# A recurrent network on one core: ScalarE instead of VectorE rounds the new state's high part in the first two blocks

## The chip, the core and the metric

The kernel runs on one core of a Trainium2 chip. The engines of the core work side by side and are tied together by semaphores only: TensorE (PE in the profile; its weight loads are PEld), VectorE (DVE), ScalarE (ACT), GpSimd (POOL, idle here) and SyncE (SP, which issues the DMAs). The metric is the time of one execution on the device in microseconds (us).

## What is computed

A gated recurrent unit runs over 128 time steps, 64 sequences side by side, with 512 inputs and 512 hidden values. After every fourth step the state that is carried on is a further layer of the new state. The result is x plus the new states. From the reference (it runs through `jax.lax.scan` over the steps):

```python
def step(h, inp):
    x_t, prop = inp
    comb = jnp.concatenate([x_t, h], axis=-1)
    z = jax.nn.sigmoid(comb @ Wz + bz)
    r = jax.nn.sigmoid(comb @ Wr + br)
    comb2 = jnp.concatenate([x_t, r * h], axis=-1)
    h_cand = jnp.tanh(comb2 @ Wh + bh)
    h_new = (1.0 - z) * h + z * h_cand
    h_next = jnp.where(prop, jnp.tanh(h_new @ Wp + bp), h_new)
    return (h_next, h_new)
...
x = x + _L0_cond_ref(x, cond_1024, ...)   # the h_new of all steps
```

## The kernel before

**Numbers as two halves.** Every factor of a product is held as a high and a low part in 16 bits: `h_split[:, :, 0]` is the state rounded to f16 and `h_split[:, :, 1]` is what is left of it. A product is then three: high weights with high values, low weights with high values, high weights with low values. The state lies transposed, as 128 partitions by 4 chunks (`KC`) by 64 sequences (`B`), 256 elements in a partition. Much is done in two halves of two chunks (`HALVES`), 128 elements each.

**The steps.** The 128 steps are 16 blocks of 8. In step t TensorE runs, in this order: the products of gate R with the state (`rec(R, ...)`, line 1122, 48 small matmuls of 64 columns, the first on the first high half), those of gate Z, those of gate C with q = r * h, and then a *fill*: part of the input products of a later block, which does not depend on the state (line 953 in block 0, 512 columns each; `stage`, line 1047, from block 1 on, 256 columns each). Then comes step t + 1. So the fill is what TensorE has to do while the other engines turn the sums of C into the new state. In steps 3, 7, 11, ... (`propagates(t)`) the further layer `PROP` is put between two pieces of fill; there the state's split goes to `q_split` (`p_split`) instead.

**ScalarE in a step** (from line 575): `squash(R)` as two halves (line 504), in steps 2, 4, 5, ... a rounding of weight sums (`split_wsum`, 465) and of input values (`split_slot`, 458), `squash(Z)` as a whole, `squash(C)` as two halves, then `seed(R, t + 1)` and `seed(Z, t + 1)`, which put the input part of the next step's sums into PSUM (524), then reading of finished fills (443, or 470 and 483), then `seed(C, t + 1)`. In step 2 `split_rec(PROP)` (498, two instructions) and the first seed of `PROP` (540) stand ahead of that. Seeds and gates are in the way of one another: an engine takes its instructions in the order written.

**VectorE in a step** (from line 859): `q_split` high as two halves (868), q in full (870), its low part (857), roundings' low parts (714, 706), `keep` = (z - 1) * h (883), `new` = z * c in halves (888), then the new state's high part `new - keep` straight to f16 in halves (898), the same difference in full precision (`h_even` or `h_odd`, 901), the low part (857), and the sum with x, which is the output (909). After that come sums for later blocks (735, 766) and magnitudes of input values (628, 631).

**Who waits.** `h_hi_ready` counts the halves of the high part; TensorE waits for 2t + 1 before the first products of step t and for 2t + 2 sixteen matmuls later. `h_lo_ready` does the same for the low part. `h_new_ready` counts the halves of the full state. Everything here is an order written out by hand; no scheduler moves anything.

## Time and profile before

| | |
|---|---|
| median of 3 runs | 1055.98 us (1055.78 to 1056.47) |
| the profiled execution's own time | 1056.31 us |
| its span in the trace | 1054.5 us |
| busy share: PE, PEld, DVE, ACT | 99%, 92%, 76%, 65% |
| granted TensorE clock | 0.999 |
| instructions: PE, DVE, ACT | 23984, 2692, 1666 |
| the recurrence starts at | 51.14 us |
| step 16 starts at | 175.09 us |

The trace counts time from the span's start. An engine's busy share does not say by itself what bounds the kernel: TensorE's matmuls are pipelined and overlap, so a matmul's duration is longer than what it adds. What it adds is the distance of two starts, 0.029 us for one of 64 columns, 0.109 us for 256 and 0.216 us for 512. PEld, the weight loads, shows better where TensorE is really held up.

### The profile page before, as it was taken

Reading aid. Unit: us, or ns where it says so; the run is one execution under the profiler, and the core shown is the slowest. Engines: PE = TensorE matmul, PEld = TensorE weight load, DVE = VectorE, ACT = ScalarE, POOL = GpSimd, SP = SyncE. Lnnn points to the kernel's source line nnn. Section 1 sums busy time; section 2 is a strip of 40 time slices with the busy share of each in tenths; the row PEclk is TensorE's granted clock in tenths of the full one; section 3 lists DMA queues with packets and bytes.
Section 4 is the critical chain, followed back from the end, with each engine's and each line's share of the span. In section 5 each row is a group of like instructions: output and inputs, shape, how many; then the busy total and the mean of one; then the engine's idle time right before and its main releaser. Section 6 shows DMA issues by size and latency. Waiting matters only on the chain.

```text
span 1054.5 us, 53898 instructions
## 1 busy us (share of the span) xinstructions
PE 1044.9 (99%) x23984; PEld 966.2 (92%) x23984; DVE 799.2 (76%) x2692; ACT 689.4 (65%) x1666; POOL 0.2 (0%) x4
## 2 busy tenths in 40 slices
PE   9999999999999999999999999999999999999997
PEld 3477999999999999999999999999999999999997
DVE  6989988877777777777777777777777776666665
ACT  4766767666666666666666666666675666565664
POOL 0000000000000000000000000000000000000000
PEclk9999999999999999999999999999999999999999
DMA  9312211101111001111001110011110000000001
GB/s 325 110 43 83 77 59 43 44 3 44 43 43 44 23 23 44 43 43 43 21 26 43 44 43 22 24 43 43 43 43 23 24 23 24 23 24 23 24 4 43
DMA packets 38344, 47.63 MB, mean 45 GB/s; under 512 B 2144, under 2 KB 33760, under 8 KB 37728
## 3 DMA queue, kind: packets, MB, share of 16 engines
q1 hardware_dynamic: 38112, 44.19, 12.4%
q8 instruction: 188, 3.08, 1.2%
q14 instruction: 44, 0.36, 0.1%
HBM read 27.40 MB, written 16.78 MB: 42 GB/s over the span
## 4 chain that ended last, share of the span: by engine, by line
PE 94%; DVE 4%; ACT 1%; DMA 1%; issue 1%; SPq 0%; DVEq 0%
PE acc L1122 54%; PE x_acc L1047 34%; PE x_acc L953 5%; PE x_acc L1072 1%; DVE mag L628 1%; DMA x_blk<-x_dram 1%; DVE wrec_lo L692 1%; DVE mag_x L631 0%; DVE win_lo L684 0%; ACT gate L504 0%; DVE x_lo L699 0%; ACT wrec_hi L498 0%; DVE x_lo L706 0%; DVE keep L883 0%; DVE x_blk L909 0%
## 5 line engine op out<-in xcount | busy, mean ns | idle before, releaser
L504 ACT ACTIVATE gate<-acc,unscale 128x128 f32<-128x128 f32 x702 | 239.0, 384 | 268.7 <-PE acc L1122 268.4
L1122 PE MATMUL acc<-h_split,wrec_hi 128*128 128x64 f16 x8192 | 343.8, 193 | 0.0
L1047 PE MATMUL x_acc<-x_hi,win_hi 128*128 128x256 f16 x1092 | 297.7, 273 | 0.0
L1047 PE MATMUL x_acc<-x_hi,win_lo 128*128 128x256 f16 x1092 | 297.6, 273 | 0.0
L1047 PE MATMUL x_acc<-x_lo,win_hi 128*128 128x256 f16 x1092 | 297.6, 273 | 0.0
L1122 PEld LDWEIGHTS acc<-h_split,wrec_hi 128*128 128x128 f16 x8192 | 283.1, 98 | 0.0
L1122 PE MATMUL acc<-q_split,wrec_hi 128*128 128x64 f16 x5088 | 215.5, 193 | 0.0
L1122 PE MATMUL acc<-h_split,wrec_lo 128*128 128x64 f16 x4096 | 203.2, 193 | 1.4 <-DVE h_split L898 1.4
L470 ACT ACTIVATE x_part<-x_acc,bias,part_unscale 128x256 f32<-128x256 f32 x312 | 159.0, 561 | 47.5 <-PE x_acc L1047 47.4
L1122 PEld LDWEIGHTS acc<-q_split,wrec_hi 128*128 128x128 f16 x5088 | 179.2, 98 | 0.0
L524 ACT ACTIVATE acc<-x_part,seed_scale 128x256 f32<-128x256 f32 x384 | 172.7, 477 | 0.1
L1122 PEld LDWEIGHTS acc<-h_split,wrec_lo 128*128 128x128 f16 x4096 | 163.0, 98 | 6.2 <-ACT acc L524 1.5
L1122 PE MATMUL acc<-q_split,wrec_lo 128*128 128x64 f16 x2544 | 126.1, 193 | 1.4 <-DVE q_split L868 1.2
L1047 PEld LDWEIGHTS x_acc<-x_hi,win_lo 128*128 128x128 f16 x1092 | 106.8, 98 | 12.4
L1047 PEld LDWEIGHTS x_acc<-x_hi,win_hi 128*128 128x128 f16 x1092 | 106.8, 98 | 11.0
L1047 PEld LDWEIGHTS x_acc<-x_lo,win_hi 128*128 128x128 f16 x1092 | 106.8, 98 | 10.9
L1122 PEld LDWEIGHTS acc<-q_split,wrec_lo 128*128 128x128 f16 x2544 | 98.0, 98 | 3.3 <-issue 2.6
L868 DVE TENSOR_TENSOR q_split<-gate,h_even 128x128 f16<-128x128 f32 x128 | 35.1, 292 | 73.4 <-ACT gate L504 73.3
L779 DVE SCALAR_TENSOR_TENSOR x_part<-x_acc,part_unscale,x_part 128x512 f32<-128x512 f32 x78 | 58.3, 749 | 30.8 <-ACT x_part L470 15.2
L888 DVE SCALAR_TENSOR_TENSOR new<-gate,scale 128x128 f32<-128x128 f32 x256 | 78.5, 348 | 0.0
L857 DVE TENSOR_TENSOR q_split<-q_full,q_split 128x128 f16<-128x128 f32 x256 | 62.3, 284 | 0.3 <-issue 0.3
L953 PE MATMUL x_acc<-x_lo,win_hi 128*128 128x128 f16 (+2 forms) x224 | 59.9, 288 | 0.0
(116 smaller groups left out, 1059.8 us busy)
## 6 DMA issues: line engine op xcount, KB each, us to landing
out_dram<-x_blk SPq DMA_DIRECT2D x30, 512.0 KB, 3.2
x_blk<-x_dram SPq DMA_DIRECT2D x24, 512.0 KB, 4.2
x_blk<-x_dram SPq DMA_DIRECT2D x3, 1024.0 KB, 8.8
x_blk<-x_dram SPq DMA_DIRECT2D x4, 256.0 KB, 4.0
x_part<-wz_dram SPq DMA_DIRECT2D x4, 256.0 KB, 7.0
x_part<-wh_dram SPq DMA_DIRECT2D x4, 256.0 KB, 6.6
x_part<-wr_dram SPq DMA_DIRECT2D x1, 1024.0 KB, 11.1
x_part<-wz_dram SPq DMA_DIRECT2D x1, 1024.0 KB, 13.3
```

Source lines behind the costliest of these rows:

```text
L470: nc.scalar.activation(part_quarter(m, g, jh, nh)[:, j], in_halves(x_acc[bank][:])[:, j], ACT.Identity, bias=bias[:, g, 2 * jh + j:2 * jh ...
L504: nc.scalar.activation(gate[g][:, half, :], acc[g][:, half, :], func, scale=unscale[:, g:g + 1]).then_inc(gate_ready[g], 1)
L524: nc.scalar.activation(acc[g], added, ACT.Copy, scale=seed_scale[:, g:g + 1]).then_inc(seed_ready[g], 1)
L628: nc.vector.tensor_reduce(mag[:, col:col + 1], src, AX_X, ALU.max, apply_absolute_value=True).then_inc(mag_ready[col], 1)
L692: nc.vector.scalar_tensor_tensor(out=flat(wrec_lo[g][:, rows]), in0=flat(stage_rec[g][:, rows]), scalar=scale[:, g:g + 1], in1=flat(wrec_h ...
L779: nc.vector.scalar_tensor_tensor(out=part_quarter(m, g, jh, 1), in0=in_halves(x_acc[bank][:]), scalar=part_unscale[:, m % 2, g:g + 1], in1 ...
L857: return nc.vector.tensor_tensor(split[:, half, 1, :], full[:, half, :], split[:, half, 0, :], ALU.subtract)
L868: nc.vector.tensor_tensor(q_split[:, half, 0, :], gate[R][:, half, :], h_in[:, half, :], ALU.mult).then_inc(q_hi_ready, 1)
L888: nc.vector.scalar_tensor_tensor(out=new[:, half, :], in0=gate[C][:, half, :], scalar=h_scale, in1=gate[Z][:, half, :], op0=ALU.mult, op1= ...
L953: return nc.tensor.matmul(x_acc[bank][:, 0:cols], weights[g][:, 2 * (j // 2) + k // 2, k % 2, j % 2 * P:(j % 2 + 1) * P], values[m % 2][:, ...
L1047: mm = nc.tensor.matmul(in_halves(x_acc[bank][:])[:, j], weights[g][:, slot_w, k, j * P:(j + 1) * P], in_halves(values[m % 2][:, slot_x, : ...
L1122: mm = nc.tensor.matmul(acc[g][:, j, :], weights[g][:, k, j * P:(j + 1) * P], values[:, k, lo, :], start=False, stop=False, skip_group_che ...
```

## The change

For the twelve steps of the first two blocks that are not followed by the further layer (steps 0, 1, 2, 4, 5, 6, 8, 9, 10, 12, 13, 14):

- VectorE does not make the high part any more (two instructions of line 898 less in each step). It makes the full state right after `new`, then adds x, then waits for both halves of the high part and makes the low part.
- ScalarE waits for both halves of the full state and makes the high part from it in one instruction of 256 elements, f32 to f16. It stands between `seed(R, t + 1)` and `seed(Z, t + 1)`, and counts `h_hi_ready` up by two at once.

In the other 116 steps nothing changes.

```diff
+        def high_by_act(t):
+
+            return t < 2 * BLOCK and not propagates(t)
...
-                if t + 1 < T:
-                    for g in (R, Z):
-                        if g not in late:
-                            seed(g, t + 1)
+                if t + 1 < T and R not in late:
+                    seed(R, t + 1)
+                if high_by_act(t):
+                    act.wait_ge(h_new_ready, 2 * t + 2)
+                    nc.scalar.copy(h_split[:, :, 0, :], h_even_odd[t % 2][:]).then_inc(h_hi_ready, 2)
+                if t + 1 < T and Z not in late:
+                    seed(Z, t + 1)
...
-                if t + 1 < T:
+                if t + 1 < T and not high_by_act(t):
                     for n, half in enumerate(HALVES):
                         dve.wait_ge(new_ready, 2 * t + n + 1)
                         nc.vector.tensor_tensor(split[:, half, 0, :], new[:, half, :], keep[:, half, :], ALU.subtract).then_inc(hi, 1)
...
+                def add_x():
+                    dve.wait_ge(h_new_ready, 2 * t + 2)
+                    nc.vector.scalar_tensor_tensor(out=x_blk[m % RING][:, :, s, :], in0=h_out[:], scalar=h_unscale,
+                                                   in1=x_blk[m % RING][:, :, s, :], op0=ALU.mult, op1=ALU.add).then_inc(out_ready, 1)
+
+                if high_by_act(t):
+                    add_x()
                 if t + 1 < T:
                     for n, half in enumerate(HALVES):
-                        dve.wait_ge(hi, count + n + 1)
+                        dve.wait_ge(hi, count + n + 1 if not high_by_act(t) else count + 2)
                         dve.wait_ge(h_new_ready, 2 * t + n + 1)
                         subtract_hi(h_out, split, half).then_inc(lo, 1)
...
+                if not high_by_act(t):
+                    add_x()
```

ScalarE around the end of step 2, before (L504 gates, L524 seeds, L498 the rounding of the further layer's weights, L540 its seed, L443 a finished fill read):

```order
33 L504 ACTIVATE gate<-acc,unscale 128x256
34 L504 ACTIVATE gate<-acc,unscale 128x128 x2
35 L524 ACTIVATE acc<-x_part,seed_scale 128x256 x2
36 L498 ACTIVATE wrec_hi<-x_blk,scale 128x1024 x2
37 L540 ACTIVATE acc<-prop_bias,seed_scale 128x256
38 L443 ACTIVATE x_part<-x_acc,bias,part_unscale 128x512
39 L524 ACTIVATE acc<-x_part,seed_scale 128x256
40 L504 ACTIVATE gate<-acc,unscale 128x128 x2
```

and after (the same lines have numbers 4 higher):

```order
37 L508 ACTIVATE gate<-acc,unscale 128x256
38 L508 ACTIVATE gate<-acc,unscale 128x128 x2
39 L528 ACTIVATE acc<-x_part,seed_scale 128x256
40 L597 CAST h_split<-h_even 128x4x64
41 L528 ACTIVATE acc<-x_part,seed_scale 128x256
42 L502 ACTIVATE wrec_hi<-x_blk,scale 128x1024 x2
43 L544 ACTIVATE acc<-prop_bias,seed_scale 128x256
44 L447 ACTIVATE x_part<-x_acc,bias,part_unscale 128x512
45 L528 ACTIVATE acc<-x_part,seed_scale 128x256
46 L508 ACTIVATE gate<-acc,unscale 128x128 x2
```

One instruction, the cast, has come in ahead of the seed of Z, and six instructions stand between it and the gate of step 3.

VectorE at the same place, before (L883 `keep`, L888 `new`, L898 the high part, L901 the full state, L857 the low part, L909 the sum with x):

```order
105 L883 SCALAR_TENSOR_TENSOR keep<-gate,h_odd 128x256
106 L888 SCALAR_TENSOR_TENSOR new<-gate,scale 128x128 x2
107 L898 TENSOR_TENSOR h_split<-new,keep 128x2x64 x2
108 L901 TENSOR_TENSOR h_even<-new,keep 128x128 x2
109 L857 TENSOR_TENSOR h_split<-h_even,h_split 128x2x64 x2
110 L909 SCALAR_TENSOR_TENSOR x_blk<-h_even,unscale,x_blk 128x4x64
```

and after:

```order
103 L890 SCALAR_TENSOR_TENSOR keep<-gate,h_odd 128x256
104 L895 SCALAR_TENSOR_TENSOR new<-gate,scale 128x128 x2
105 L908 TENSOR_TENSOR h_even<-new,keep 128x128 x2
106 L911 SCALAR_TENSOR_TENSOR x_blk<-h_even,unscale,x_blk 128x4x64
107 L864 TENSOR_TENSOR h_split<-h_even,h_split 128x2x64 x2
```

The full state has moved up to the place of the high part, and the sum with x ahead of the low part.

ScalarE at the end of step 8, the first of block 1, before (L483 copies a finished product within PSUM, L470 reads another one as two halves):

```order
86 L524 ACTIVATE acc<-x_part,seed_scale 128x256 x2
87 L483 COPY x_acc<-x_acc 128x512
88 L470 ACTIVATE x_part<-x_acc,bias,part_unscale 128x256 x2
89 L524 ACTIVATE acc<-x_part,seed_scale 128x256
90 L504 ACTIVATE gate<-acc,unscale 128x128 x2
```

and after:

```order
98 L528 ACTIVATE acc<-x_part,seed_scale 128x256
99 L597 CAST h_split<-h_even 128x4x64
100 L528 ACTIVATE acc<-x_part,seed_scale 128x256
101 L487 COPY x_acc<-x_acc 128x512
102 L474 ACTIVATE x_part<-x_acc,bias,part_unscale 128x256 x2
103 L528 ACTIVATE acc<-x_part,seed_scale 128x256
104 L508 ACTIVATE gate<-acc,unscale 128x128 x2
```

The cast stands ahead of five instructions that lead up to the gate of step 9.

## Rows read from the trace of the kernel before

**Rows 1.** The page: busy time and share of the span; the chain's shares by engine

```profile
PE 1044.9 (99%) x23984; PEld 966.2 (92%) x23984; DVE 799.2 (76%) x2692; ACT 689.4 (65%) x1666; POOL 0.2 (0%) x4
PE 94%; DVE 4%; ACT 1%; DMA 1%; issue 1%; SPq 0%; DVEq 0%
```

**Rows 2.** Busy time of each engine in stretches of 15 us

```profile
core 0: us, PE busy (x) PEld busy (x) DVE busy (x) ACT busy (x) POOL busy (x), PEclk, DMA share, GB/s
90.00:105.00 15.00, 14.59 (x345) 11.61 (x341) 15.00 (x46) 11.29 (x26) 0.00 (x0) 1.00 0.25 74
195.00:210.00 15.00, 15.00 (x365) 14.38 (x364) 11.76 (x43) 10.57 (x26) 0.00 (x0) 1.00 0.19 62
```

**Rows 3.** Timeline, step 1: start, us, engine, line, xcount [idle before <-releaser]

```profile
60.13 0.62 ACT L504 ACTIVATE gate<-acc,unscale 128x128 f32<-128x128 f32 x2 [0.49 <-PE acc L1122]
60.65 0.48 DVE L868 TENSOR_TENSOR q_split<-gate,h_even 128x128 f16<-128x128 f32 x2
```

**Rows 4.** Timeline of step 2

```profile
67.04 0.63 ACT L504 ACTIVATE gate<-acc,unscale 128x128 f32<-128x128 f32 x2 [0.48 <-PE acc L1122]
67.62 0.48 DVE L868 TENSOR_TENSOR q_split<-gate,h_odd 128x128 f16<-128x128 f32 x2
```

**Rows 5.** Timeline from the end of step 2 to the C products of step 3

```profile
70.70 0.49 DVE L898 TENSOR_TENSOR h_split<-new,keep 128x128 f16<-128x128 f32 x2
70.28 0.87 ACT L524 ACTIVATE acc<-x_part,seed_scale 128x256 f32<-128x256 f32 x2
71.08 2.18 ACT L498 ACTIVATE wrec_hi<-x_blk,scale 128x1024 f16<-128x1024 f32 x2
74.62 0.61 ACT L504 ACTIVATE gate<-acc,unscale 128x128 f32<-128x128 f32 x2
75.02 0.54 DVE L868 TENSOR_TENSOR q_split<-gate,h_even 128x128 f16<-128x128 f32 x2 [0.21 <-ACT gate L504]
75.45 0.39 PE L1122 MATMUL acc<-q_split,wrec_lo 128*128 128x64 f16 x8 [0.45 <-DVE q_split L868]
```

**Rows 6.** Instructions of ScalarE by form, 48 to 170 us: xcount, busy us, mean ns

```profile
L504 ACT ACTIVATE gate<-acc,unscale 128x128 f32<-128x128 f32 x69 | 21.6, 364 | 13.3 <-PE acc L1122 13.1
L524 ACT ACTIVATE acc<-x_part,seed_scale 128x256 f32<-128x256 f32 x47 | 21.1, 476 | 0.0
L470 ACT ACTIVATE x_part<-x_acc,bias,part_unscale 128x256 f32<-128x256 f32 x20 | 10.2, 560 | 3.0 <-PE x_acc L1047 3.0
L465 ACT ACTIVATE win_hi<-sum_b,scale 128x512 f16<-128x512 f32 x6 | 4.3, 718 | 0.0
L483 ACT COPY x_acc<-x_acc 128x512 f32<-128x512 f32 x3 | 1.7, 568 | 1.2 <-PE x_acc L1047 1.2
```

**Rows 7.** Timeline from the end of step 5 to the start of step 6

```profile
93.81 0.49 DVE L898 TENSOR_TENSOR h_split<-new,keep 128x128 f16<-128x128 f32 x2
94.90 0.37 PE L1122 MATMUL acc<-h_split,wrec_lo 128*128 128x64 f16 x7
```

**Rows 8.** Timeline from step 6 to the C products of step 7

```profile
97.22 0.48 DVE L868 TENSOR_TENSOR q_split<-gate,h_odd 128x128 f16<-128x128 f32 x2
101.28 0.48 DVE L898 TENSOR_TENSOR h_split<-new,keep 128x128 f16<-128x128 f32 x2
101.75 0.40 PE L1122 MATMUL acc<-h_split,wrec_lo 128*128 128x64 f16 x8
103.58 0.63 ACT L504 ACTIVATE gate<-acc,unscale 128x128 f32<-128x128 f32 x2 [0.49 <-PE acc L1122]
104.69 0.48 DVE L868 TENSOR_TENSOR q_split<-gate,h_even 128x128 f16<-128x128 f32 x2
105.11 0.36 PE L1122 MATMUL acc<-q_split,wrec_lo 128*128 128x64 f16 x7 [0.52 <-DVE q_split L868]
```

**Rows 9.** Timeline from the end of step 8 to the gate of step 9

```profile
117.24 0.48 DVE L898 TENSOR_TENSOR h_split<-new,keep 128x128 f16<-128x128 f32 x2
117.80 0.40 PE L1122 MATMUL acc<-h_split,wrec_lo 128*128 128x64 f16 x8
116.73 0.57 ACT L483 COPY x_acc<-x_acc 128x512 f32<-128x512 f32 x1
118.00 1.02 ACT L470 ACTIVATE x_part<-x_acc,bias,part_unscale 128x256 f32<-128x256 f32 x2 [0.71 <-PE x_acc L1047]
119.64 0.62 ACT L504 ACTIVATE gate<-acc,unscale 128x128 f32<-128x128 f32 x2 [0.24 <-PE acc L1122]
```

More of the change, by code:

```diff
@@ L901, in _ @@
                     nc.vector.tensor_tensor(h_out[:, half, :], new[:, half, :], keep[:, half, :], ALU.subtract).then_inc(h_new_ready, 1)
+                def add_x():
[4 more added lines that the diff above has]
+                    add_x()
                 if t + 1 < T:
                     for n, half in enumerate(HALVES):
-                        dve.wait_ge(hi, count + n + 1)
+                        dve.wait_ge(hi, count + n + 1 if not high_by_act(t) else count + 2)
                         dve.wait_ge(h_new_ready, 2 * t + n + 1)
                         subtract_hi(h_out, split, half).then_inc(lo, 1)
-                else:
-                    dve.wait_ge(h_new_ready, 2 * t + 2)
-                nc.vector.scalar_tensor_tensor(out=x_blk[m % RING][:, :, s, :], in0=h_out[:], scalar=h_unscale,
-                                               in1=x_blk[m % RING][:, :, s, :], op0=ALU.mult, op1=ALU.add).then_inc(out_ready, 1)
+                if not high_by_act(t):
+                    add_x()
                 if m + 2 < BLOCKS and s == scale_at(m + 2):
```

## The prediction, as it was put on record

> **What bounds the kernel now.** I read the page's busy times and the chain of waits first. The chain that ended last lies on TensorE for 94% and on VectorE for 4% of the span, and the weight loads are busy for 92% [rows 1]. So the time is TensorE's own stream of work, plus the few places at which that stream stands still. Next I read the stretches. From 195 to 210 us, behind the changed steps, the weight loads are busy for 14.38 of 15 us: TensorE is full. From 90 to 105 us, in block 0, VectorE is busy for all 15 us, and the weight loads for 11.61 (partly because that fill has 512 columns for each load) [rows 2]. VectorE is the tight engine there. Yet what counts is where TensorE waits, and that is read from the timeline of its matmuls. The two large standstills ahead of step 16 that come from the state's loop stand before the C products of steps 3 and 7: TensorE is idle for 0.45 and 0.52 us in the page's terms [rows 5, 8]. Measured from start to start, less the 0.029 us that a 64-column matmul takes, it is about 0.61 and 0.68 us. Everything that makes such a place longer or shorter in the first two blocks moves the end by the same amount, since nothing behind them has slack to give.
>
> The two places have different causes. In step 3 the gate of R comes late (74.62 us) because ScalarE works through a row of instructions without a pause, the two roundings L498 of 2.18 us among them. VectorE had been idle for 0.21 us when the gate came [rows 5]. In step 7 the gate had been there since 103.58 us plus 0.36, and q started only at 104.69: VectorE was late by its own queue [rows 8].
>
> **Handing over.** From a gate to q: the first half of the gate starts at 60.13 and takes 0.364 us [rows 3, 6], and q can follow after 0.03 us. In step 3 q follows 0.40 us behind the gate's start; I use 0.40. From VectorE to TensorE: 0.14 us in step 3 (75.02 + 0.29 for one half of q, then 75.45) [rows 5]; I use 0.15, also from ScalarE to TensorE, which no row shows. From VectorE to ScalarE no row of the loop shows it either; I take 0.04, as from ScalarE to VectorE, and 0.15 as the far end.
>
> **The cast's price K.** No row shows a cast on ScalarE. Seeds have the same 256 elements and take 476 ns with one scale operand; L470 has a bias as well and takes 560, so an operand costs some 85 ns, and the cast has none: 476 - 85 = 0.39 us. L483, a copy without operands, takes 568 ns for 512 elements; from 128 to 256 elements gate and seed differ by 112 ns, so that 256 fewer would take off 0.22, leaving 0.35. Bounds: 0.30 below, and 0.57 above, what the copy of twice the size takes; the farthest row, 512 elements from SBUF to SBUF in f16, takes 718 ns [rows 6]. I take 0.39, nearest to the seed's row, which reads SBUF as the cast does. The next instruction of ScalarE starts some 0.08 us before the one ahead ends, as two seeds do (two in 0.87 us, 0.476 each) [rows 5, 6]. On this price the Trainium skill ("VectorE: DVE Perf Modes", section on the TRN2 errata) speaks against many small ScalarE instructions: SBUF sources pay a fixed cost each, 224 cycles plus one per element at 1.2 GHz; an estimate from that page is 480 cycles = 0.40 us, and the sum below would be 0.03 us more. No run so far shows the cast itself.
>
> **When the high part is there now.** The full state takes the place of the high part, so its two halves are done when those of L898 were. Then come 0.04 to ScalarE, K, and 0.15 to TensorE, together 0.19 + K = 0.58 us. What hides this is the fill. Its reserve is the start of the next step's first matmul minus the end of L898. Of the twelve steps it is about 0.96 to 1.06 us in steps 0, 1, 2 and 4 (step 2: L898 ends at 71.19), 1.94 in steps 9, 12 and 14, and 0.60 to 0.64 in steps 5, 10 and 13, of which step 5 is shown (94.90 - 94.30) [rows 5, 7]. In step 6 it is 101.75 - 101.76 = -0.01 and in step 8 it is 117.80 - 117.72 = 0.08 [rows 8, 9]. The first ten are covered, three of them by only 0.02 to 0.06 us; the last two are not.
>
> **The sum, place by place.**
>
> *Steps 1 and 2: a small gain.* q starts at 60.65 and 67.62, while the gates at 60.13 and 67.04 would allow 60.53 and 67.44 [rows 3, 4]. VectorE was late by a magnitude and by scales in its queue, and it now has two instructions of 0.20 us each less ahead of them (0.40 in all for the pair's place). So these gaps go: C starts about 0.09 and 0.17 us earlier. The first is smaller than 0.12, because TensorE's own stream was ready only 0.09 before. Together -0.26 us.
>
> *Step 2 to 3: a loss.* ScalarE had seeded R from 70.28 and Z from 70.68, and started the roundings at 71.08. Now the cast may start only at 71.19 + 0.04 = 71.23, so Z's seed starts at 71.23 + 0.39 - 0.08 = 71.54, 0.86 us later than before. Behind it stand L498 twice, the seed of PROP, a fill's reading, the seed of C and the gate of R for step 3, all back to back [rows 5]. TensorE waits for q, which waits for that gate. The whole 0.86 us is added to the standstill at 75.45. In terms of K: 0.47 + K. Most of it, 0.55 us, is waiting for the full state, not casting.
>
> *Steps 6 and 7: one gap for another.* Step 7's first product comes at 101.76 + 0.58 = 102.34, 0.59 late. VectorE's relief does not help here: q of step 6 was let go by its gate and everything from there to the new state stands behind it [rows 8]. The gate of step 7 is then at 103.58 + 0.59 = 104.17, q at 104.57 instead of 104.69. Before, q was late by VectorE's queue; that queue is about 0.1 shorter now (0.40 saved, 0.3 given back waiting for the cast before the low part). So the gap before C shrinks by more than the new one costs: -0.12, or K - 0.51. Here the old standstill is the cover.
>
> *Steps 8 and 9: a loss.* Step 9 starts at 117.72 + 0.58 = 118.30, 0.50 late, and no old gap takes it up. ScalarE is also behind: the cast starts at 117.76, Z's seed at 118.07, then L483 (0.48 from start to start), L470 twice (0.92) and C's seed (0.40), each seed 0.40. So the gate of R could start at 118.07 + 2.20 = 120.27, while TensorE would allow 119.64 + 0.50 = 120.14 [rows 9]. That is 0.13 more: 0.63 in all, or 0.24 + K.
>
> *The other steps:* nothing on TensorE; the cast and the later Z seed lie beside the fill and the first products of R. The low part comes 0.3 us later or less, and TensorE asks for it 0.9 us behind the first product. No DMA moves on SP's queue; the output's sum is ready earlier.
>
> Sum: -0.26 + 0.86 - 0.12 + 0.63 = **+1.11 us**; with K free, -0.06 + 3K. With K = 0.30 it is 0.8; with 0.57 it is 1.65, and steps 5, 10 and 13 then miss their reserve by some 0.1 each, 2.0 in all. A handover of 0.15 to ScalarE instead of 0.04 adds 0.3. Against the profiled execution's 1056.31 us that is 1057.4; against the median of the runs, which lies 0.33 lower, it is **1057.1 us**.
>
> **Rivals.**
>
> *The relief of the tight engine wins.* VectorE is at 15.00 of 15 us in block 0 [rows 2], loses 12 x 0.40 = 4.8 us of work, and its lateness costs TensorE 0.26 us in steps 1 and 2 and 0.68 in step 7. If the casts disappeared behind the fill, the sum would be -0.9: 1055.1. Against it: the reserve of step 6 is nil and ScalarE has no pause in step 2. The Trainium skill ("Perfetto Trace Analysis", section on optimizing Scalar/DVE operations) has this as a rule: with a saturated VectorE it may make sense to move work to ScalarE. The trace agrees that VectorE is saturated there, but shows the state's path running through both engines. Chance 0.06.
>
> *It changes nothing.* The change is in 12 of 128 steps, and if the handovers are shorter than I took and old gaps absorb the new ones, as in step 7, it is 0 to 0.5 us: 1056.2. Against it: step 9 has no gap to absorb anything. That the change does not do what it says is no separate case: the order shows twelve casts more and 24 subtractions fewer. Chance 0.12.
>
> *The cast is dear.* If it costs what a 512-element rounding takes, 0.72 us, -0.06 + 3K gives 2.1, and the reserves of 0.60 to 0.64 in steps 5, 10 and 13 are missed by about 0.3 each: 3.0 in all, 1059.0, slower beyond what can be told from none. This decides from K of about 0.57 on. For it: no cast was ever seen here, and its f16 output is strided. Against it: gates and seeds agree on a price by element. Chance 0.10.
>
> **How the numbers follow.** The forecast, between 0.7 and 2.0 us of loss, has 0.72. The range takes in the rivals at 1056.2 and, nearly, those at 1055.1 and 1059.0, with the runs' own spread of 0.7 us: 1055.4 to 1058.7. A measurement of this kernel can tell about 0.2%, 2.1 us, from no change. Of the forecast and both lower rivals nearly all lies within that: same 0.88. Slower is the dear cast, 0.10. Faster by 2.1 us would need more than all the standstills that the loop's waits make, 0.02.
>
> **What would show it.** In the profile after: casts of 0.39 us; the C products of step 3 starting 0.6 us later than 75.45, ahead of them step 3 itself earlier by some 0.26; a new wait before the first product of step 7 and none of note before its C products; the same before step 9; from step 10 on a constant shift of about 1.1 us to the end. Wrong would be a shift that grows in steps 10 to 14 (the cast is dear), or one that is negative at step 16 (the relief wins).

## The result and the profile after

The changed kernel takes 1058.38 us (median of 20 runs, 1057.82 to 1058.97), the kernel before, run beside it, 1056.57 us (20 runs, 1055.78 to 1057.18). The ratio is 1.0017, with a 95% interval of 1.0011 to 1.0023: 1.8 us slower, between 1.2 and 2.4. The forecast was 1057.1 us, a loss of 1.1. Of the 1.3 us between forecast and median, 0.6 is no error on the change: the median of before, over 20 runs, lies 0.6 above that of the 3 runs from which the forecast started. The rest, some 0.7 us, is looked for below.

The page of after, its busy times and the chain's shares (in the place of [rows 1]):

```profile
PE 1045.2 (99%) x23984; PEld 966.0 (91%) x23984; DVE 798.0 (76%) x2668; ACT 695.5 (66%) x1678; POOL 0.2 (0%) x4
PE 94%; DVE 3%; ACT 1%; DMA 1%; issue 1%; SPq 0%; ACTq 0%; DVEq 0%
```

VectorE has 24 instructions less and ScalarE 12 more. Their busy time in the stretch of the change, 48 to 170 us (columns as in [rows 2]), before:

```profile
48.00:170.00 122.00, 120.61 (x2789) 104.15 (x2788) 111.33 (x350) 86.24 (x198) 0.00 (x0) 1.00 0.18 57
```

and after:

```profile
48.00:170.00 122.00, 118.97 (x2736) 102.05 (x2735) 107.82 (x321) 88.95 (x207) 0.00 (x0) 1.00 0.18 57
```

VectorE, the tight engine, is busy for 3.5 us less and ScalarE for 2.7 more, and TensorE's weight loads for 2.1 less: TensorE got less done in the same 122 us, so part of the 3.5 us is work that now falls behind the stretch. From the start of step 0 to the start of step 16, the same work in both traces, VectorE is busy for 112.59 us before and 110.62 after, and ScalarE for 85.87 and 90.11: 2.0 us less and 4.2 more. The granted clock is 1.00 in both. The work was moved as said, and the time rose all the same. Where it rose is seen in TensorE's waits. The standstills that TensorE has from 48 to 165 us, by what it waits for (engine, line, waited for: us in total, times, longest), before:

```profile
PE acc L1122 <- DVE q_split L868: 1.2, 3, 0.5
```

and after:

```profile
PE acc L1134 <- DVE q_split L875: 1.6, 2, 1.4
PE acc L1134 <- ACT h_split L597: 0.9, 2, 0.5
PE acc L1134 <- DVE q_split L905: 0.4, 1, 0.4
```

The small waits of steps 1 and 2 are gone, one wait for q has grown to 1.4 us, there are two waits for the cast, and one, for line 905, which the forecast did not have.

To add them up I set the two traces side by side, with the first product of gate R of each step (R) and its first C product (C) as marks, counted from the start of step 0. The table has after minus before in us:

| mark | after - before | place | measured | forecast |
|---|---|---|---|---|
| C of step 2 | -0.25 | steps 1, 2 | -0.25 | -0.26 |
| C of step 3 | +0.67 | step 2 to 3 | +0.92 | +0.86 |
| R of step 7 | +1.35 | first product of 7 | +0.64 | +0.59 |
| C of step 7 | +0.67 | steps 4 to 7, net | 0.00 | -0.12 |
| R of step 8 | +0.96 | within step 7 | +0.29 | 0 |
| R, C of step 9 | +1.53, +1.64 | step 8 to 9 | +0.57, +0.11 | +0.50, +0.13 |
| C of step 14 | +1.76 | step 13 to 14 | +0.11 | 0 |
| R of step 16 | +1.62 | step 15 to 16 | -0.14 | 0 |

The row of step 7's first product counts from R of step 6 (+0.71) and is contained in the net row below it. The sum is 1.62 us at the end of block 1, against 1.11. It stays there within 0.1 us as far as step 60. In this one execution it then grows to 1.94 by step 126; in the kernels below it changes over the same steps by 0.2 us or less. The cause of this growth is open.

**The casts.** ScalarE by form, 48 to 170 us (line, shapes, xcount, busy us, mean ns, idle before), to be read against [rows 6]:

```profile
L597 ACT CAST h_split<-h_even 128x256 f16<-128x256 f32 x8 | 3.3, 407 | 7.0 <-DVE h_even L908 7.0
```

A cast takes 407 ns, where I had put 0.39 us. The estimate of 0.40 us from the Trainium skill ("VectorE: DVE Perf Modes", the TRN2 errata) was nearer by a hair; the trace agrees with that page's price for an SBUF source.

**Step 2 to 3** (timeline: start, us, engine, line, xcount, idle before), in the place of [rows 5]:

```profile
70.53 0.49 DVE L908 TENSOR_TENSOR h_even<-new,keep 128x128 f32<-128x128 f32 x2
71.11 0.41 ACT L597 CAST h_split<-h_even 128x256 f16<-128x256 f32 x1 [0.51 <-DVE h_even L908]
71.42 0.47 ACT L528 ACTIVATE acc<-x_part,seed_scale 128x256 f32<-128x256 f32 x1
71.83 2.18 ACT L502 ACTIVATE wrec_hi<-x_blk,scale 128x1024 f16<-128x1024 f32 x2
75.38 0.61 ACT L508 ACTIVATE gate<-acc,unscale 128x128 f32<-128x128 f32 x2
75.77 0.55 DVE L875 TENSOR_TENSOR q_split<-gate,h_even 128x128 f16<-128x128 f32 x2 [0.21 <-ACT gate L508]
76.20 0.28 PE L1134 MATMUL acc<-q_split,wrec_lo 128*128 128x64 f16 x4 [1.37 <-DVE q_split L875]
```

Read it from the top. The full state ends at 70.53 + 0.49 = 71.02 and the cast starts at 71.11, so the handover is 0.09 us and not 0.04. ScalarE had nothing to do for 0.51 us ahead of the cast, though a seed and two long roundings stood behind it. Then it works on without a pause to the gate at 75.38, which was at 74.62. TensorE waits 1.37 us for q instead of 0.45.

**Steps 6 and 7**, in the place of [rows 8]:

```profile
102.62 0.41 ACT L597 CAST h_split<-h_even 128x256 f16<-128x256 f32 x1 [1.39 <-DVE h_even L908]
103.17 0.39 PE L1134 MATMUL acc<-h_split,wrec_lo 128*128 128x64 f16 x8 [0.54 <-ACT h_split L597]
...
107.97 0.61 DVE L895 SCALAR_TENSOR_TENSOR new<-gate,scale 128x128 f32<-128x128 f32 x2
108.78 0.49 DVE L905 TENSOR_TENSOR q_split<-new,keep 128x128 f16<-128x128 f32 x2 [0.19 <-DVE new L895]
109.22 0.25 PE L1134 MATMUL acc<-q_split,wrec_lo 128*128 128x64 f16 x3 [0.39 <-DVE q_split L905]
```

TensorE now stands before the first product of step 7, as forecast, and not before its C products. But further down there is something new. `new` ends at 107.97 + 0.61 = 108.58, and the next instruction of VectorE starts at 108.78. Before, the same two instructions of step 7 stood like this:

```profile
107.22 0.61 DVE L888 SCALAR_TENSOR_TENSOR new<-gate,scale 128x128 f32<-128x128 f32 x2
...
107.76 0.48 DVE L898 TENSOR_TENSOR q_split<-new,keep 128x128 f16<-128x128 f32 x2
```

From start to start that is 0.54 us before and 0.81 us after. Nobody else is late: L905 needs only `new` and `keep`, both made by VectorE itself. The profile writes the idle time down to `new`, whose last half ended 0.20 us earlier. The products of the further layer wait for this, and the 0.29 us never come back.

**Step 8 to 9**, in the place of [rows 9]:

```profile
118.85 0.41 ACT L597 CAST h_split<-h_even 128x256 f16<-128x256 f32 x1 [1.39 <-DVE h_even L908]
119.40 0.39 PE L1134 MATMUL acc<-h_split,wrec_lo 128*128 128x64 f16 x8 [0.41 <-ACT h_split L597]
...
120.04 1.03 ACT L474 ACTIVATE x_part<-x_acc,bias,part_unscale 128x256 f32<-128x256 f32 x2
120.96 0.48 ACT L528 ACTIVATE acc<-x_part,seed_scale 128x256 f32<-128x256 f32 x1
121.36 0.63 ACT L508 ACTIVATE gate<-acc,unscale 128x128 f32<-128x128 f32 x2
```

The cast starts late and TensorE waits for it; behind it ScalarE is busy without a pause up to the gate at 121.36, and this costs the other 0.11 us.

### The profile page after: what moved, and what is told of

It is laid out like the page before. It is cut to its first block, busy times and chain, and to the rows that moved or that the text cites. A ratio compares the mean times of both kernels' runs of the same rounds, so it can differ in the third digit from the quotient of the medians.

```text
span 1056.5 us, 53898 instructions
## 1 busy us (share of the span) xinstructions
PE 1045.2 (99%) x23984; PEld 966.0 (91%) x23984; DVE 798.0 (76%) x2668; ACT 695.5 (66%) x1678; POOL 0.2 (0%) x4
## 4 chain that ended last, share of the span: by engine, by line
PE 94%; DVE 3%; ACT 1%; DMA 1%; issue 1%; SPq 0%; ACTq 0%; DVEq 0%
PE acc L1134 54%; PE x_acc L1059 34%; PE x_acc L965 5%; PE x_acc L1084 1%; DVE mag L635 1%; DMA x_blk<-x_dram 1%; DVE wrec_lo L699 1%; ACT gate L508 0%; DVE win_lo L691 0%; DVE x_lo L713 0%; DVE keep L890 0%; DVE x_lo L706 0%; DVE new L895 0%; ACT wrec_hi L502 0%; DVE mag_x L638 0%
## 5 line engine op out<-in xcount | busy, mean ns | idle before, releaser
L965 PE MATMUL x_acc<-x_hi,win_hi 128*128 128x128 f16 (+2 forms) x224 | 59.9, 288 | 0.0
```

The lines of the kernel that those rows point to most:

```text
L965: return nc.tensor.matmul(x_acc[bank][:, 0:cols], weights[g][:, 2 * (j // 2) + k // 2, k % 2, j % 2 * P:(j % 2 + 1) * P], values[m % 2][:, ...
```

## The experiments

My theory: the loss is made at three places only (into step 3, step 7 and step 9), where no fill covers "full state, cast, handover", and it comes from the hop to ScalarE and from what is queued there, not from the cast's arithmetic. Rivals: a small cost at each of the 12 steps; a cost of the cast itself wherever it is made; and, for the 0.29 us in step 7, an effect of this step's work, or one of nothing but the place that an instruction has in VectorE's program. The shifts below are marks of an experiment's trace minus those of before, aligned at the start of step 0 as in the table above. The medians named as before are of the runs on the same chip.

### One step at a time: 2, 6, 8

```diff
-            return t < 2 * BLOCK and not propagates(t)
+            return t == 2
```

> The change in step 2 alone. Theory A (the loss is made of a few places at which the state's path or ScalarE's queue has no reserve, and they add up): nothing before the C products of step 3, these 0.9 us later than before (in the full change they moved from 0.18 early to 0.75 late, 0.93), constant from there to the end: +0.9 us. Rival B (each of the twelve steps costs about the same, 1.7 us / 12): +0.15 us.

Measured: 1057.09 us against 1056.33 (one run each). The shift is +0.89 at the C products of step 3 and stays there as far as step 15; at step 16 it is 0.81, since a small standstill that before has there is half as long.

```profile
76.33 0.39 PE L1134 MATMUL acc<-q_split,wrec_lo 128*128 128x64 f16 x8 [1.35 <-DVE q_split L875]
```

One step's cast alone makes the whole 1.35 us standstill before the C products of step 3. That is the place with the largest price.

```diff
-            return t < 2 * BLOCK and not propagates(t)
+            return t == 6
```

> The change in step 6 alone. Theory A: the first product of step 7 about 0.65 us late, its C products 0.0 to 0.05 us early, since the old standstill of 0.68 us there is used up; no new wait of VectorE of 0.28 us before the high part of step 7, if that wait came from where the instructions lie in the program; nothing at the end. If the wait of 0.28 us in step 7 belongs to the cast in step 6 instead, it shows here, and the end is +0.3 us. Rival B: +0.15 us.

Measured: 1056.46 us against 1056.33. The first product of step 7 is 0.63 late, and its C products 0.11. The old gap takes up all of the 0.63 and 0.04 more; then 0.15 us are lost in the middle of TensorE's stream, with no wait that the profile names:

```profile
102.54 0.55 PE L1134 MATMUL acc<-h_split,wrec_lo 128*128 128x64 f16 x8 [0.48 <-ACT h_split L597]
102.92 0.40 PE L1134 MATMUL acc<-h_split,wrec_hi 128*128 128x64 f16 x8
```

Eight products of one group go from 102.54 to 102.92, 0.38 us, where they take 8 x 0.029 = 0.23 everywhere else. Step 7 of this kernel has no standstill of VectorE before the further layer, though it has the same late start as after. So the 0.29 us do not belong to step 6's cast.

```diff
-            return t < 2 * BLOCK and not propagates(t)
+            return t == 8
```

> The change in step 8 alone. Theory A: the first product of step 9 0.57 us late, its C products 0.68 us late (ScalarE's queue adds 0.1), constant to the end: +0.7 us. Rival B: +0.15 us.

Measured: 1056.66 us against 1056.33. The first product of step 9 is 0.54 late, its C products 0.64, and this stays as far as step 15; at step 16 it is 0.56.

The terms of the sum, each alone: 0.89, -0.04 (with the break left out) and 0.64. Those of the full change are 0.92, 0.00 and 0.68. The places are independent of one another, and the terms add up.

### All steps but these three

```diff
-            return t < 2 * BLOCK and not propagates(t)
+            return t < 2 * BLOCK and not propagates(t) and t not in (2, 6, 8)
```

> The change in the nine steps 0, 1, 4, 5, 9, 10, 12, 13, 14, without 2, 6 and 8. Theory A: C of step 1 0.1 us and C of step 2 0.27 us early, nothing lost at step 3, 7 or 9, perhaps 0.1 us lost at step 14: -0.2 us at step 16, less than can be told by timing. Rival B: 9/12 of the loss, +1.3 us.

Measured: 1056.37 us against 1056.33. The shift is -0.26 at the C products of step 2, -0.21 at those of step 7, -0.11 at those of step 14, and -0.26 at step 16. The standstill into step 3 is left as it was, 0.48 us in the profile's terms against 0.45 [rows 5]. Nine of the twelve casts are covered, and by them the kernel gains the small amount of steps 1 and 2, 0.26 us. That is below what the runs' medians can show, so the trace alone shows it. The rival "a small cost at every step" falls. One of the nine does cost: the cast of step 13, 0.10 us, although its fill covers it. By step 16 this is made up for by something that has nothing to do with casts (the place in the program, below).

### The cast on VectorE

VectorE makes the high part from the full state itself, ahead of the sum with x; ScalarE is as it was before.

```diff
-                if high_by_act(t):
-                    act.wait_ge(h_new_ready, 2 * t + 2)
-                    nc.scalar.copy(h_split[:, :, 0, :], h_even_odd[t % 2][:]).then_inc(h_hi_ready, 2)
...
                 if high_by_act(t):
+                    dve.wait_ge(h_new_ready, 2 * t + 2)
+                    nc.vector.tensor_copy(h_split[:, :, 0, :], h_out[:]).then_inc(h_hi_ready, 2)
                     add_x()
```

> The changed order, but VectorE casts from the full state itself (one instruction of 256 elements, right behind the full state); ScalarE is as before. It parts what the new order costs from what the other engine costs. Theory A: nothing lost at step 3 (that loss was ScalarE's queue), the first product of step 7 about 0.4 us late and made good by the old standstill, the first product of step 9 about 0.35 us late: +0.3 to +0.5 us. Rival C (handing over between the engines is the whole loss, the order costs nothing): 0.0.

Measured: 1057.07 us against 1056.33. C of step 3: +0.02 (after: +0.67). R of step 7: +0.58, C of step 7: +0.01. Step 9: +0.48. At step 16: +0.60, of which 0.1 is a break in TensorE's stream at 122.31, without a wait.

```profile
75.42 0.39 PE L1133 MATMUL acc<-q_split,wrec_lo 128*128 128x64 f16 x8 [0.48 <-DVE q_split L872]
```

and by form, 48 to 170 us:

```profile
L913 DVE CAST h_split<-h_even x8: 294/294/295, 57.4 to 164.1; 128x256 f16<-128x256 f32 x8
```

This kernel keeps the way through the full state but has no ScalarE in it. Into step 3 nothing is lost, as the fill covers this path there: so the 0.92 us there are ScalarE's queue, that is the cast and the wait for the full state ahead of all that stands behind them. Into steps 7 and 9 nearly as much is lost as with ScalarE, 0.58 of 0.64 and 0.48 of 0.57: there it is the additional step on the state's path that costs. That it costs nearly as much with 294 ns instead of 407 has its reason in this row and the one of the cast:

```profile
101.23 0.49 DVE L905 TENSOR_TENSOR h_even<-new,keep 128x128 f32<-128x128 f32 x2
101.83 0.29 DVE L913 CAST h_split<-h_even 128x256 f16<-128x256 f32 x1
```

VectorE waits for its own result, from 101.72 to 101.83, 0.11 us. With 0.29 for the cast and 0.15 to TensorE the path is 0.55 us long, against 0.09 + 0.41 + 0.14 = 0.64 by ScalarE.

### The cast twice

A second cast, which waits for the first, counts `h_hi_ready` up.

```diff
+                    nc.scalar.copy(h_split[:, :, 0, :], h_even_odd[t % 2][:]).then_inc(first_cast, 1)
+                    casts[0] += 1
+                    act.wait_ge(first_cast, casts[0])
                     nc.scalar.copy(h_split[:, :, 0, :], h_even_odd[t % 2][:]).then_inc(h_hi_ready, 2)
```

> The full change, with the cast done twice in a row, so that the high part comes 0.44 us later in each of the twelve steps. Theory A: steps 3, 7 and 9 each lose 0.4 us more, and the reserves of 0.60 us in steps 5, 10 and 13 (against 0.64 needed now, 1.08 then) are missed by 0.48 us each, those of 0.96 to 1.06 in steps 0, 1, 2, 4 by about 0.1; some is taken up: about +5 us to before, +3.4 to the change. Rival B (the same price in each step, in proportion to the cast): +3.4 us to before. Rival D (the fill hides the cast but for step 3): +2.1 us.

Measured: 1061.53 us (4 runs, 1061.12 to 1061.85) against 1056.33 (7 runs); ratio 1.0048, 1.0031 to 1.0065. In the trace +5.33 us at step 16, 3.7 more than the change. With the cast once more on the path, steps that were covered are not:

```profile
97.61 0.39 PE L1138 MATMUL acc<-h_split,wrec_lo 128*128 128x64 f16 x8 [0.26 <-ACT h_split L601]
...
71.93 0.41 ACT L598 CAST h_split<-h_even 128x256 f16<-128x256 f32 x1 [0.46 <-DVE h_even L912]
72.42 0.41 ACT L601 CAST h_split<-h_even 128x256 f16<-128x256 f32 x1
```

The second cast starts 0.49 us behind the first. The path grows by this and the reserve of 0.60 to 0.64 us in steps 5, 10 and 13 is gone ([rows 7] has step 5), with waits of 0.26 to 0.28 us there besides what follows in the queue. This is what the rival "the cast is dear" would have looked like: +0.5 us on the path costs some 3.7 us, because the number of steps that are not covered goes from 3 to more. At 407 ns the change stands just short of that edge: 0.64 us needed, 0.60 to 0.64 there.

### Both seeds ahead of the cast

```diff
+                if t + 1 < T and Z not in late:
+                    seed(Z, t + 1)
                 if high_by_act(t):
                     act.wait_ge(h_new_ready, 2 * t + 2)
                     nc.scalar.copy(h_split[:, :, 0, :], h_even_odd[t % 2][:]).then_inc(h_hi_ready, 2)
-                if t + 1 < T and Z not in late:
-                    seed(Z, t + 1)
```

> The full change, but ScalarE seeds both R and Z before it waits for the full state. Theory A: the seed of Z fills the time in which ScalarE waits, so the C products of step 3 come 0.40 us earlier than in the full change and those of step 9 0.11 us earlier; the first products of steps 7 and 9 are as late as there. About 0.5 us less than the change at step 16: +1.1 us. Rival E (ScalarE's queue is no cause, the late high part is all): as the change, +1.6 us.

Measured: 1057.96 us against 1056.33 (7 runs). C of step 3 is at +0.25, which is 0.42 less than after:

```profile
71.18 0.41 ACT L599 CAST h_split<-h_even 128x256 f16<-128x256 f32 x1
...
75.86 0.39 PE L1134 MATMUL acc<-q_split,wrec_lo 128*128 128x64 f16 x8 [0.96 <-DVE q_split L875]
```

Counted from the start of step 0 the cast starts when it did in after (its own time, 71.18 against 71.11, is later only because the whole recurrence starts 0.08 us later here), and the pause ahead of it is filled with the seed. So of the 0.92 us, 0.42 was a seed that stood behind a wait for a result that it does not need; the rest is the cast and the remaining wait. Step 14 loses nothing here (+1.57 at step 9's C products as at step 14's): the 0.11 us there were ScalarE's queue. But the gain is eaten in step 7: from its C products (+0.27) to R of step 8 (+0.95) 0.68 us are lost, that is 0.28 from the same standstill on VectorE as after, and 0.40 from a break in TensorE's stream:

```profile
106.62 0.28 PE L1134 MATMUL acc<-q_split,wrec_hi 128*128 128x64 f16 x4
107.13 0.48 PE L1134 MATMUL acc<-q_split,wrec_hi 128*128 128x64 f16 x11 [0.23 <-issue]
```

The profile names no releaser for it ("issue"). Altogether +1.43 us at step 16.

### Sixteen instructions more ahead of VectorE's program

What have the standstills of VectorE in common? In the records of VectorE (instructions and semaphore waits counted together) they are at 576 before (a wait; the instruction is 577), 320 after, 448 with step 2, 6 or 8 alone, 192 without these three and with the cast on VectorE, 320 with the cast twice and with both seeds first. All are 64 + a multiple of 128. So the theory is that VectorE starts the instruction at such a place some 0.28 us late, if nothing else makes it wait there, and that the change moved such a place onto the path of step 7 by the number of its instructions. The rival: the work of step 7 itself. The test adds 16 tiny instructions at the very beginning, some 50 us before the recurrence, and changes nothing else. (A kernel with 24 of them gave no time: the tensor that they write needs 96 bytes in each partition of SBUF, and 92 were free.)

```diff
+            for n in range(16):
+                nc.vector.memset(pad[:, n:n + 1], 0.0)
```

> The full change, with 16 small instructions on VectorE at the very front of the kernel, before any data have come, which do nothing. They shift all that follows on VectorE by 16 places in the program. In the change the high part of step 7 started 0.28 us later than its inputs explain, and it stood behind record 320 = 5 x 64 of VectorE; in the kernels with one step changed the same delay stands behind record 448 = 7 x 64. Theory F (it comes from the place in the program): step 7 has no such delay, the further layer's products there wait 0.27 us as before and not 0.56, and step 16 comes 0.3 us earlier than in the change, +1.3 us (with a delay of the kind perhaps elsewhere). Rival G (it belongs to the work of steps 6 and 7): the delay is still there, +1.6 us.

Measured: 1058.5 us (one run) against 1056.38 (15 runs); the memsets take 0.28 us, and the recurrence starts 0.56 us later than in before, which is in this time. Counted from the start of step 0 the shift is +0.68 at C of step 7 as in after, and still +0.68 at R of step 8, where after has +0.96. At step 16 it is +1.30 instead of +1.62.

```profile
108.47 0.61 DVE L898 SCALAR_TENSOR_TENSOR new<-gate,scale 128x128 f32<-128x128 f32 x2
...
109.00 0.48 DVE L908 TENSOR_TENSOR q_split<-new,keep 128x128 f16<-128x128 f32 x2
```

From `new` to the high part: 0.53 us, as in before, not 0.81. The standstill of step 7 is gone, by 16 instructions at another end of the program and with the same work in step 7. So it belongs to the place in the program. This is one kernel, and its recurrence also starts 0.48 us later than in after; but the place speaks for itself here too: step 11 now has the standstill, at 140.26 us, and that is record 448, 64 + 3 x 128. The same goes for the gain of 0.14 us from step 15 to 16: there the kernel before has a standstill of this kind at its record 576, which after has not:

```profile
172.36 0.29 DVE L857 TENSOR_TENSOR q_split<-h_odd,q_split 128x128 f16<-128x128 f32 x1 [0.16 <-issue]
```

### A version with the reserve made ahead of it

If the theory holds, casts should be where the fill covers them, and what ScalarE does in step 2 should be out of the way. This version casts on ScalarE in steps 0, 1 and 2 only, behind both seeds; the first half of the further layer's rounding (`split_rec`) goes ahead of `squash(Z)` in step 2; one magnitude of block 3's input goes from step 6 to step 7, out of VectorE's queue ahead of step 7's q; and in steps 3 and 7 one more piece of fill stands ahead of the further layer.

```diff
-SEVEN_MAG_AT = {2: (1, 1, 3, 3), 3: (-4, -3, -2, -1)}
+SEVEN_MAG_AT = {2: (1, 1, 3, 3), 3: (-4, -3, -1, -1)}
...
-        return first, (first + issued(t)) // 2, issued(t)
+        return first, (first + issued(t)) // 2 + (t in (3, 7)), issued(t)
...
+                if t == 2:
+                    split_rec(PROP, HALVES[:1])
...
-                    split_rec(PROP)
+                    split_rec(PROP, HALVES[1:])
...
+            return t < 3
```

> What the runs point to, put on the kernel before: the cast on ScalarE in steps 0, 1 and 2 alone, behind both seeds; the first of the two roundings of the further layer's weights taken from the end of step 2 to ScalarE's pause ahead of the gate of Z there, so that the gate of R of step 3 is not held up; one magnitude of VectorE moved from step 6 to step 7; in steps 3 and 7 one matmul of the fill moved ahead of the further layer's products, which wait 0.27 us there. Theory A, place by place: -0.26 by the C products of step 2, about -0.36 more at step 3 (then VectorE's roundings hold), -0.21 at step 4, -0.60 at the C products of step 7, -0.21 at step 8: -1.6 us, ratio 0.9985. Rival B (time is spread over the twelve steps, no single place matters): under -0.5 us.

Measured: 1054.79 us (11 runs, 1054.48 to 1056.44) against 1056.38 (15 runs); ratio 0.9988, 0.9979 to 0.9997. The gain is 0.12%, below the 0.2% that I called distinguishable, and the interval only just leaves out 1. In the trace it is -0.58 at C of step 3, -0.79 at R of step 4, -1.39 at C of step 7, -1.60 at R of step 8, -1.74 at step 16.

```profile
68.09 1.14 ACT L502 ACTIVATE wrec_hi<-x_blk,scale 128x1024 f16<-128x1024 f32 x1
...
71.07 0.41 ACT L601 CAST h_split<-h_even 128x256 f16<-128x256 f32 x1 [0.15 <-DVE h_even L910]
71.38 1.15 ACT L502 ACTIVATE wrec_hi<-x_blk,scale 128x1024 f16<-128x1024 f32 x1
...
73.90 0.60 ACT L508 ACTIVATE gate<-acc,unscale 128x128 f32<-128x128 f32 x2
```

and what is left of the waits of TensorE, 48 to 165 us:

```profile
PE acc L1136 <- DVE q_split L877: 0.2, 1, 0.2
```

Instead of 1.2 us there are 0.2. The five edits were not run apart; by their places, the cast in steps 0 and 1 gave 0.26, step 2's rounding with its cast 0.32, the fill of steps 3 and 7 0.21 each, and the 0.60 between step 4 and the C products of step 7 falls where the magnitude was. These are 1.60; the other 0.14 comes from step 15 to 16, as in after, and is the place in the program. What the change itself was made for, the relief of VectorE, is 0.26 of the 1.74.

## Why the prediction was right, and where its terms were off

**The likeliest case came.** No gain from relieving the tight engine, a loss of 1.6 us in the trace where 1.11 was summed, at the places named, and a constant shift from step 16 on. The median, 1058.38, is within the range.

**Steps 1 and 2: right** (-0.26 summed, -0.25 measured, and -0.26 in the kernel without steps 2, 6 and 8).

**Step 2 to 3: right in mechanism, 0.06 too small.** The handover from VectorE to ScalarE is 0.09 us, where I had taken 0.04 from the opposite direction; the cast is 0.407 for 0.39. That the cast came so near is partly luck: I took 85 ns for an operand from L470 and the seed, and these differ in more than an operand, since L470 reads its values from PSUM and the seed from SBUF. The far end that I kept, 0.15, would have been too much. My sentence that most of this is waiting and not casting holds: ScalarE stands idle for 0.51 us ahead of the cast, and filling that with the seed takes 0.42 off. The cast on VectorE takes all of it off and does not part the two.

**Steps 6 and 7: right in mechanism, 0.12 too good.** The first product was late by 0.64 (0.59 forecast), and the gap before C, gone whole, took up 0.68 of it: -0.04. Step 5's reserve of 0.60, missed by the longer path of 0.64, cost 0.03 ahead of step 6, which makes the sum nothing. My -0.12 was more than my own numbers allowed: it set q's start 0.12 earlier, but TensorE's own stream, ready at 105.11 - 0.68 + 0.59 = 105.02, would not have let C start more than 0.09 earlier. Once the stream is last, relieving q's queue brings nothing. One reading was wrong besides: I wrote that q of step 6 was let go by its gate. The gate there starts at 96.74 us before, and q at 97.22, 0.48 us behind it and not 0.40: VectorE's queue held it for 0.08. In after it is 0.40 (97.52 and 97.92), and C of step 6 gains 0.06 on its first product. The new state gains only 0.01 of it, so nothing of this reaches the sum.

**Steps 8 and 9: right** (0.63 summed as 0.50 and 0.13, 0.68 measured as 0.57 and 0.11).

**"The other steps: nothing": this step of the prediction failed**, by +0.26 us in all. Two things were in it. ScalarE's queue from step 13 to 14 costs 0.11 us, though the cast is covered by the fill: five instructions follow one another without a pause up to the gate, just as in step 9, and I had looked for this only where the first product is late. The rows that show it in after, with no idle time in front of any behind the first:

```profile
158.46 0.41 ACT L597 CAST h_split<-h_odd 128x256 f16<-128x256 f32 x1 [0.87 <-DVE h_odd L908]
158.77 0.47 ACT L528 ACTIVATE acc<-x_part,seed_scale 128x256 f32<-128x256 f32 x1
159.19 0.54 ACT L487 COPY x_acc<-x_acc 128x512 f32<-128x512 f32 x1
159.65 1.02 ACT L474 ACTIVATE x_part<-x_acc,bias,part_unscale 128x256 f32<-128x256 f32 x2
160.57 0.48 ACT L528 ACTIVATE acc<-x_part,seed_scale 128x256 f32<-128x256 f32 x1
160.97 0.37 ACT L508 ACTIVATE gate<-acc,unscale 128x128 f32<-128x128 f32 x1
```

Then the place of VectorE's instructions: +0.29 in step 7 and -0.14 at step 15, together +0.15. This could not be read from the change; the trace of before has the effect once ahead of step 16, at 172.36 us, and I had not seen it, since I read waits and this is none. These two and the 0.06, 0.12 and 0.05 of the places above all lie on the same side and make up the 0.5 us between 1.11 and 1.62. Nor did VectorE's relief bring the end anything in steps 4 to 14.

**The rivals.** "The relief wins" has fallen: where the casts are covered it brings 0.26 us, and nothing more. Its 4.8 us of work less on VectorE were not there either, for its busy time from step 0 to step 16 fell by 2.0 us. The durations of its instructions add up to 5.6 us less (138.3 and 132.7), but they also overlap by 3.8 us less: two that follow one another directly overlap by some 0.08 us, and there are 279 such pairs where there were 332. The rule of the Trainium skill ("Perfetto Trace Analysis", optimizing Scalar/DVE operations), that with a saturated VectorE it may make sense to offload to ScalarE, did not pay here: VectorE was at 15.00 of 15 us [rows 2], yet what counts is a path that runs from VectorE to ScalarE to TensorE. "It changes nothing", 0 to 0.5 us, has fallen: the interval begins at 1.2 us. "The cast is dear" did not come at 407 ns, and the kernel with two casts showed that its mechanism was real: another 0.49 us on the path brings 3.7 us.

**What is left open.** Between the trace's 1.6 us at step 16 and the medians' 1.8 there is 0.2 us, and the profiled execution shows a growth of 0.3 us after step 16, most of it after step 60. No experiment was made on it. Two others show half of it between steps 16 and 126 (+0.15 and +0.18, with the padding and in the last version).

## What to carry to other kernels

In this kernel, taking work off a saturated engine did not pay where that work lay on a dependent chain: the chain paid a handover and a queue at each change, 0.64 us for an operation of 0.41, and only where TensorE had more other work than this did it vanish. Before moving such an instruction, list for each step the reserve (start of the next product minus end of its input), then look at what stands behind the new instruction in its new queue: a wait blocks all that follows it, so put work that needs nothing from the wait ahead of it. And read the timeline for gaps that have no reason, too, since adding or taking away instructions shifts them about.

## What was not expected of the hardware

**At one record in 128 VectorE can start an instruction some 0.3 us late, for no reason that the profile shows.** In the first two blocks and just behind them it is seen at records 192, 320, 448, 576, 704 and 832: after at 108.78, before at 172.36, and in the kernel of steps 0 to 14 without 2, 6 and 8 like this:

```profile
72.13 0.29 DVE L864 TENSOR_TENSOR h_split<-h_even,h_split 128x128 f16<-128x128 f32 x1 [0.27 <-issue]
```

It is not seen at each such record: over the 128 steps 7 of 27 in before and 9 of 26 in after start over 0.1 us later than the same instruction does elsewhere; at most of the others VectorE works on without a pause. In the kernel with the cast on VectorE the cast at record 192 starts 0.36 us later than the other casts do (0.47 behind the full state instead of 0.11), but the fill covers it. Sixteen instructions at the front of the program moved one off the path of step 7. The traces speak for the fetch of instructions, though no run forced it on its own. The profile of after has two DMA queues that carry instructions (packets, MB, share of the 16 engines):

```profile
q8 instruction: 188, 3.08, 1.2%
q14 instruction: 43, 0.35, 0.1%
```

That is 16 KB for each packet of the one and 8 KB for each of the other. The Trainium skill ("Runtime: NRT & Kernel Launch", instruction fetch mechanics) says that an engine's instructions come ahead of their use over a DMA queue, in 16 KiB blocks of 256. By the size that this gives for one instruction a packet of q14 holds 128, an estimate, and this is the period seen on VectorE; one of q8 holds 256, as on TensorE below. The page calls the cost of a block's border mostly hidden; here some 0.3 us is in the open at times, if this is it.

The times of the packets fit. In before and in after each of the 27 and 26 records 64 + 128k of VectorE from step 0 on has an 8 KB packet of q14 that starts within 2.1 us of it; halfway between these records the nearest one is 15 to 17 us away in the median. Where the standstill is seen, the packet mostly starts 0.6 to 0.7 us behind the late instruction; where it is not, often up to 2 us ahead of it. Behind the late instruction of step 7, from 108.7 to 110 us of after, there is one, and in the 3.7 us ahead of it none:

```profile
q14 instruction: 1, 0.01, 1.9%
```

**TensorE has such breaks too**, of 0.07 to 0.40 us, in the middle of a group of products and with no wait: in the runs with step 6 alone, with the cast on VectorE, with the cast twice, with both seeds first, and in the last version. In the first two blocks all lie at records 194 or 195 + a multiple of 256 (products and weight loads counted together). The same records of other runs show none. No run forced or moved one on purpose, so their cause stays open, and there is none in the first two blocks of the kernel before or of the change. They make single-place differences of 0.1 to 0.4 us between two kernels hard to attribute.

**Handovers.** From VectorE to ScalarE 0.09 us, from either to TensorE 0.15, from ScalarE to VectorE 0.03. The cast of 256 elements, f32 to f16, takes 294 ns on VectorE and 407 on ScalarE.
